# Output tail of a conditioned-attention and recurrence kernel: three parts summed in memory, one more summed by TensorE, and new instruction orders

## What is computed

```
y    = x @ W[itok7].T + b[itok7]                      # a weight matrix per sequence
q,k,v = y @ Wq.T + bq, ...                             # 16 heads of 16
sim  = q.k / (4 * temp)
score = sum over 5 frequencies of alpha * sin(2 pi sim / freq + phi)
w    = sigmoid(score); w = w / sum(w)                  # no softmax
a    = layernorm(w.v @ Wo.T + bo) * gamma + beta
x1   = x + a                                           # residual
h    = relu(x1 @ W1[itok8] + b1); x2 = x1 + h @ W2[itok8] + b2
z    = layernorm(x2) * gamma[itok8] + beta[itok8]
for t in range(32):                                    # over the sequences
    f, i = sigmoid(z[t] @ wf.T + c @ uf.T + bf), sigmoid(... wi, ui, bi)
    c = f * c + i * tanh(z[t] @ wc.T + c @ uc.T + bc)
out  = x1 + tanh(z @ wo.T + c_last @ uo.T + bo)
```

## Time and profile before

| | us |
|---|---|
| median of 3 runs | 320.94 (320.41 to 322.8) |
| the profiled execution | 323.39 |
| its span (first to last instruction) | 321.6 |
| busy: PE, DVE, ACT | 285.4, 274.6, 257.3 |
| granted TensorE clock, mean | 0.983 |

### The profile page before, as it was taken

The page is one execution under the profiler, slowest core; times in us unless marked ns, Lnnn a source line. Parts: engine busy times, 40 slices in busy tenths (PEclk is TensorE's granted clock), DMA queues, the critical chain, the costliest instruction groups (busy, mean ns, idle before and its releaser), DMA issues.

```text
span 321.6 us, 7374 instructions
## 1 busy us (share of the span) xinstructions
PE 285.4 (89%) x2686; PEld 177.5 (55%) x2686; DVE 274.6 (85%) x598; ACT 257.3 (80%) x378; POOL 51.6 (16%) x58
## 2 busy tenths in 40 slices
PE   0787898969889989999999998899999999998971
PEld 0576647866546855554575645556665545543350
DVE  3049996999999999999999998999999998554265
ACT  1069998999999999999999999899999894422132
POOL 5000600041100012332100214140013331210000
PEclk9999997998999999999999999999999999999997
DMA  5698427544044248045445240330444160020007
GB/s 174 244 388 303 93 30 227 116 135 67 0 91 117 30 113 242 0 75 118 103 88 143 74 68 1 71 70 15 108 106 67 35 150 16 2 34 2 0 0 261
DMA packets 32374, 31.97 MB, mean 99 GB/s; under 512 B 10706, under 2 KB 24274, under 8 KB 32338
## 3 DMA queue, kind: packets, MB, share of 16 engines
q1 hardware_dynamic: 27410, 26.67, 29.1%
q0 software_dynamic: 4352, 4.20, 8.7%
q10 hardware_dynamic: 576, 0.64, 0.8%
HBM read 23.36 MB, written 2.10 MB: 79 GB/s over the span
## 4 chain that ended last, share of the span: by engine, by line
DVE 39%; PE 32%; ACT 14%; issue 8%; DMA 3%; POOL 2%; SPq 1%; DVEq 0%; ACTq 0%; POOLq 0%
DVE sc L1626 12%; PE pg L694 7%; DVE ang L1615 5%; PE pg L685 5%; DVE ang L1606 5%; ACT ang L1130 4%; PE pf L491 3%; PE pav L589 3%; ACT ang L1139 3%; PE pf L571 2%; PE pf L547 2%; DVE fc L1761 2%; ACT sc L1121 2%; DMA w<-x 1%; DVE vz L1596 1%
## 5 line engine op out<-in xcount | busy, mean ns | idle before, releaser
L1139 ACT ACTIVATE ang<-ang,qs 128x2560 f32<-128x2560 int32 x32 | 77.4, 2433 | 0.3 <-DVE ang L1615 0.2
L1626 DVE SCALAR_TENSOR_TENSOR sc<-ang,ratio,sc 128x512 f32<-128x512 f32 (+1 forms) x120 | 73.0, 637 | 0.4
L1130 ACT ACTIVATE ang<-sc,phase 128x512 int32<-128x512 f32 (+1 forms) x110 | 64.5, 650 | 0.0
L685 PE MATMUL pg<-gate_w,zT 128*64 128x384 f32 x256 | 50.8, 499 | 0.6 <-DVE zT L1751 0.4
L694 PE MATMUL pg<-gate_u,cT 128*64 128x384 f32 x256 | 47.7, 493 | 1.6 <-DVE cT L1770 1.5
L1615 DVE TENSOR_SCALAR ang<-ang 128x2560 int32<-128x2560 int32 x32 | 47.5, 1501 | 0.0
L1606 DVE TENSOR_SCALAR ang<-sc,phase 128x256 int32<-128x256 f32 (+1 forms) x90 | 32.4, 412 | 2.6 <-ACT sc L1121 2.5
L1179 ACT ACTIVATE gat<-pg 128x384 f32<-128x384 f32 x32 | 15.6, 487 | 22.7 <-PE pg L694 22.3
L694 PEld LDWEIGHTS pg<-gate_u,cT 128*64 128x64 f32 x256 | 16.4, 136 | 22.1 <-issue 15.0
L513 PE MATMUL pf<-wc,xg 128*64 128x256 f32 x128 | 17.1, 416 | 9.5 <-DMA wc<-in_cond 8.8
L1149 ACT ACTIVATE sc<-sc,lead 128x512 f32<-128x512 f32 (+1 forms) x40 | 23.4, 628 | 2.3 <-DVE sc L1626 2.2
(11 more groups left out here) (114 smaller groups left out, 474.1 us busy)
## 6 DMA issues: line engine op xcount, KB each, us to landing
wc<-in_cond SPq DMA_DIRECT2D x30, 257.0 KB, 3.5
w<-in_up SPq DMA_DIRECT2D x32, 128.5 KB, 2.6
wa<-in_down SPq DMA_DIRECT2D x32, 66.0 KB, 1.9
xt<-in_xt SPq DMA_DIRECT2D x8, 256.0 KB, 3.0
xt<-rows POOLq DMA_DIRECT2D x8, 256.0 KB, 4.2
w<-x POOLq DMA_DIRECT2D x8, 256.0 KB, 4.2
xg<-in_x SPq DMA_DIRECT2D x3, 512.0 KB, 5.1
qm<-qT SPq DMA_DIRECT2D x48, 32.0 KB, 2.1
```

The source lines that it names most:

```text
L685: pe.matmul(pg[n % 2][u * L:(u + 1) * L, 0:GCOLS], zT[:, q % 2, kc, t * L:(t + 1) * L], gate_w[:, kc, u, :], start=False, stop=(kc == KC - ...
L1130: op = act.activation(ang[:, n % SLOTS, f, r], unit(n)[:, r], ACT.Identity, scale=TURN / FREQS[f], bias=phase[:, p * NF + f:p * NF + f + 1])
L1139: act.activation(a.bitcast(F32), a, ACT.Sin, scale=2 * PI_LOW / TURN, bias=qs[:, 3:4]).then_inc(sine_ready, 1)
L1626: op = dve.scalar_tensor_tensor(out=unit(n)[:, r], in0=ang[:, n % SLOTS, f, r].bitcast(F32), scalar=ratio[:, p * NF + f:p * NF + f + 1], i ...
```

## The change

Four things change in one step.

- **Tail, in memory.** For parts 0, 5 and 1 (`OUT_DMA`) SP stores x1 into the output inside the recurrence (`store_x1`). At the end the tanh of these parts isn't added to x1 by VectorE: POOL adds it to the output in HBM with an accumulating transfer (`out_added`).
- **Tail, by TensorE.** Part 5 joins parts 6 and 7 as one whose sum with hoc TensorE makes: its kept product is brought back into PSUM (`bring_back`) and `output_sum(5)` adds hoc. The output parts 6 and 7 are made ahead of `state_output` rather than behind it. The order of the tanh is 0, 5, 1, 2, 6, 3, 7, 4.
- **Small moves between engines.** `ON_ACT` loses one angle of the units 10, 12 and 21 and gains one of unit 22, so VectorE makes two angles more. The bias row of part 6 comes from TensorE (`output_bias(6)`) rather than ScalarE. Gate biases by TensorE: cells 13, 21 and 28 added, 17 and 24 taken out.
- **New orders** on all five lists. The 9 rest constants are loaded behind the attention constants and the first weights of group 1, the adapter weights of part 0 behind the second `spread_q`, and `centre_output_weights` on VectorE moves from after the first `divided` to the beginning.

```diff
-BIAS_BY_PE = (0, 1, 2, 4, 6, 8, 10, 12, 14, 16, 17, 18, 24, 31)
-ROW_BY_PE = (0, 1, 2, 3, 4, 5)
+BIAS_BY_PE = (0, 1, 2, 4, 6, 8, 10, 12, 13, 14, 16, 18, 21, 28, 31)
+ROW_BY_PE = (0, 1, 2, 3, 4, 5, 6)
...
-BY_PE = (6, 7)
-BY_DVE = (0, 1, 2, 3, 4, 5)
-TAIL = (0, 1, 2, 3, 4, 5, 6, 7)
+BY_PE = (5, 6, 7)
+BY_DVE = (0, 1, 2, 3, 4)
+OUT_DMA = (0, 5, 1)
+TAIL = (0, 5, 1, 2, 6, 3, 7, 4)
+STORED = tuple(q for q in TAIL if q not in OUT_DMA)
...
+            def store_x1(q):
+
+                added_wait(sp, q)
+                sp.dma_start(out[part(q)].rearrange("u p d -> p u d"), x1[:, part(q)]).then_inc(x1_out, 16)
...
+            def out_added(q):
+
+                pool.wait_ge(x1_out, 16 * len(OUT_DMA))
+                pool.wait_ge(tail_tanh, TAIL.index(q) + 1)
+                pool.dma_start(out[part(q)].rearrange("u p d -> p u d"), kept(q), accum_op=ALU.add).then_inc(summed_out, 16)
...
+            def bring_back(q):
+
+                pe.wait_ge(go_kept, q + 1)
+                pe.wait_ge(s_copied, B)
+                pe.wait_ge(v_ready, NG)
+                pe.matmul(banks[q], eye[:, :], flat(go[:, part(q)]), start=True, stop=False, skip_group_check=True)
...
+            output_part(7, 0)
+            output_part(7, 1)
+            state_turned(31)
+            bring_back(5)
+            state_output()
+            output_sum(5)
+            output_sum(6)
+            output_sum(7)
```

822 lines of the change are left out of this document (409 added, 413 removed).

## The result

| | median | runs | profiled execution | span |
|---|---|---|---|---|
| before, beside after | 321.87 us | 4, 320.41 to 324.05 | 323.39 us | 321.6 us |
| after | 326.9 us | 4, 326.27 to 330.42 | 327.07 us | 325.2 us |

The ratio of after to before on record is 1.0191, 95% interval 1.0136 to 1.0246: some 6 us (4.4 to 7.9). The prediction had nothing, and its range ended at +2.5. Of the forecast cases none happened; the nearest, A, had the right sign and part of the mechanism.

What follows compares the result with a forecast made beforehand. VectorE's work was taken to bound 64 to 263 us, recurrence and TensorE 263 to 308, then VectorE's tail. Terms -1.50 + 0.96 - 0.90 + 1.05 + 0.30 = -0.09 gave 320.8 us from median 320.94; 8-in-10 range 317.2 to 323.4.

Steps and rivals of the forecast that it cites:

- A: Rival at the end: accumulating transfers into HBM take 3.0 us each and land last; +4.7, 325.5 us; chance 0.09.
- First groups, -1.50: Start, 51 to 56 us: centring output weights earlier fills VectorE's hole, so angles start sooner; -1.5 us, bounds 0 and 2.5.
- Two angles, +0.96: 64 to 263 us: net two 128x512 angles move to VectorE, 0.48 us each, lengthening that stretch by 0.96 us.
- POOL's wait goes, -0.90: 64 to 263 us: new orders remove VectorE's one listed wait, for POOL's deviation of part 4; -0.90 us.
- new waits 0: All steps may wait somewhere new under the new orders; taken as 0, with ends of +2 and -1.8 us.
- the prediction's own sign: 64 to 263 us: VectorE idling more than 4 us there would mean the forecast is wrong.
- Warm matmuls, 0: TensorE's early waits: removed or added idle matmuls stand in waits and change nothing.
- End of the recurrence, +1.05: Last cells from 26: TensorE's moved pieces overfill its windows; +1.05 us, between 0.3 and 2.0, including +0.41 for bringing part 5 back.
- The bound of 2.0: End of the recurrence: upper cost in us if weight loads of 0.1 to 0.2 are exposed at each piece.
- Tail, 8.25 us behind hoc: After hoc starts: VectorE's last addition ends 8.25 us later, before 9.05; only 0.8 us of 2.5 dropped comes back.
- Draining, +0.30 together with the tail: Last stores: serial transfers end 12.35 us after hoc starts (T), +0.65; if accumulating costs nothing, -0.8; taken +0.30.

Runs made afterwards that it cites:

- g1: f3 with the angles of units 10 and 12 given back from VectorE to ScalarE; 324.73 us, ratio 1.0069.
- f2: Changed kernel with four places of VectorE's list altered: three normalising steps and a residual moved relative to neighbouring work; 326.40 us, ratio 1.0145.
- f3: f2 with the tail of the kernel before and its order at cell 26, without the gate bias of cell 28 on TensorE; 323.37 us, ratio 1.0055.
- e1: Changed kernel with the whole tail of the kernel before, other new lists kept; 325.04 us, ratio 1.0092.
- g3: Kernel before with only TensorE's part of the new tail, no early stores or accumulating transfers; 323.70 us, ratio 1.0033.
- e2: Kernel before with the whole new tail and early stores, all other lists as before; 324.99 us, ratio 1.0076.
- h3: Kernel before without the two warm matmuls ahead of the first queries; 322.42 us, ratio 1.0010.
- h1: Changed kernel with the two warm matmuls ahead of the first queries put back; 326.31 us, ratio 1.0130.
- h2: f3 with the two warm matmuls ahead of the first queries put back; 322.65 us, ratio 1.0035.
- f4: Kernel before with only parts 0 and 1 stored early and their tanh added by accumulating transfers; 322.71 us, ratio 0.9997.
- g2: Kernel before with unit 24's wrap ahead of part 3's second moments and part 3's normalising ahead of part 4's residual; 322.50 us, ratio 1.0002.
- e4: Changed kernel with output parts 6 and 7 behind state_output and input gates of cells 28 and 31 whole ahead of the turn; 326.85 us, ratio 1.0126.

## Why the prediction was wrong, point by point

- *First groups, -1.50.* Right in place, and at first larger than predicted: the first large angle starts at 52.90 us instead of 56.26, unit 4's sine 2.2 us sooner (59.60 for 61.79). But the lead is gone by cell 26: 289.23 in both profiles. It was a lead over an order that then had less idle time. This and the next two points are the largest miss: ahead of cell 26 the prediction's terms come to -1.44 us, and it was +1.4 to +2.5.
- *Two angles, +0.96.* g1 found nothing of it, within its noise. A cost per instruction holds only while that engine is the bound.
- *POOL's wait goes, -0.90; new waits 0.* This step failed, and the prediction's own sign of it came: VectorE idled 5.6 us from 64 to 263, where over 4 was to mean a wrong forecast. The wait of part 4 only moved, and three more of over 0.5 us for POOL came, 0.93 + 0.71 + 0.59 + 0.62 = 2.85 us for 0.90, and one of 1.01 us for the adapter's accumulating transfer of part 5 (0.60 to 1.03 in eight of the ten profiles of the changed lists, in none of the six of the lists of before):

```profile
248.49 0.69 DVE L1737 TENSOR_TENSOR w<-pr,w 128x512 f32<-128x512 f32 x1 [1.01 <-DMA w<-x]
```

  The orders were on the table: a wrap behind `moments(0, 1)` could be read from the list, and the wait of the earlier trace rows itself had such a wrap ahead of it (POOL's instruction took 1.35 us at 195.87 in the kernel before, 0.22 at 82.87). I put the wait down to an order and asked neither why POOL was late nor what work stood between it and the step that waits. How much of the 1.4 to 2.5 us this is: f2 gives 0.46% by ratios (1.5 us), 0.9 by the medians and 0.5 us by the profile, f3 against e1 some 0.9 us beside cell 26. I estimate 0.5 to 1.5 us from these; none of them is clear of the noise by itself.
- *Warm matmuls, 0.* Failed in kind: where the clock had risen by then, they kept it up. In size it is 0.3 to 1.0 us by the medians, not clear of the noise.
- *End of the recurrence, +1.05.* The way of counting was right, the sizes too small, and with them one step wrong in kind: 2.46 us. Half an output part is 1.06 us, taken as 0.86; half of the input gates 0.80, taken as 0.64. Together they were to fit the first window, at nothing; they overran it by 0.41 us at two cells. Cell 28's second half costs 0.19, as predicted, and the last cell, with its half of the gates and part 7, 0.57 for 0.36. The order at cell 26 costs 0.53 behind the turn (22.32 for 21.79; a net 0.25 by e1), taken as 0.1. `bring_back` was right: hoc followed the last turn by 2.21 us where it was 1.86, +0.35 for +0.41. The bound of 2.0 that I gave for exposed loads of weights was still too low.
- *Tail, 8.25 us behind hoc.* 7.93, right.
- *Draining, +0.30 together with the tail.* Failed in size. One transfer after the other was to end the data at T + 12.35, and I then took less than half of the +0.65. The last full window ends at 324, T + 12.45, but 28% of the next is still used, so the data ends near T + 12.7 by the measure that gave 11.7 before; the trace's last packet ends at T + 12.96 (T + 11.71 in the kernel before). That the serial count comes near is in part luck: it had 1.55 us for an accumulating transfer, which was 1.86, and its first data at T + 3.85, which was T + 4.3, and the engines' share went up to 1.19 in a window, where it had counted 1. From hoc to the end of the span it is 13.65 us where it was 12.51, +1.14. The rule of the Trainium skill that the prediction quoted, "DMA: Bandwidth & Descriptors", section "Issuing engines are not separate DMA queues", that all transfers end up on the same 16 engines, made it +0.65 and was the better number; the trace agrees, with stores landing in 5.2 us beside accumulating transfers where they took 2.3 without.
- *Rival A.* It had the accumulating transfers land last. The third lands at T + 12.43, 8.4 us after its issue, and the last store, which shares the engines with it, at T + 13.28. They take 1.86 us each, above the 1.6 from which the rival was to decide and far from its 3.0. Of its 4.7 us, 0.7 to 1.0 came (T + 12.7 to 12.96 for T + 12.0).
- *The range.* Its upper end, 323.4, is 0.3 us more than its own terms give (320.8 + 0.95 + 0.35 + 1.0 = 323.1); the result lies outside by either.

Sum by the runs, in per cent of the time. By the runs alone each difference is near its noise; the profiles behind the turn of cell 26 bear out the first three, and the last two stand on the runs: TensorE's pieces 0.3 (g3), accumulating transfers 0.4 (e2 less g3), order at cell 26 0.1 (e1, net), the four places 0.3 to 0.5 (f3, f2), warm 0.1 to 0.3 (h3, h1 and h2, by their medians). Together 1.2 to 1.6 of 1.9 (1.6 by the medians). What h2 still has, 0.35% (0.05 to 0.66) or about 1 us (0.6 by the medians), stays open: it lies ahead of cell 26, in lists that differ at some hundred places, and no single one was found for it. The wait for part 5's transfer, 0.73 us in h2, is a candidate, which wasn't tried apart.

No kernel that ran beats the kernel before; f4, g2 and h3 equal it within what the runs tell.

## What to carry to other kernels

An engine at 98% of a stretch is a statement on one order. When an order changes, don't price only the work moved: for each step that waits on another engine, ask what now runs *beside* the small instruction it waits for, and how much of its own work stands between. Where a full window is to take one more piece, measure the piece by its starts in a full stretch. And when work is moved to the DMA engines at the end of a program, price the end of the data, not the end of the compute: what VectorE saved here (1.1 us behind hoc) the engines took back twice (2.3 us).

## What was not expected of the hardware

- A GpSimd `tensor_scalar` on 128x2 numbers takes 0.22 us alone (276.87 in the kernel before), 0.62 beside a VectorE sum of 128x512 with two inputs in SBUF, 1.36 beside an int32 `tensor_scalar` of 128x2560, and 2.02 beside the end of such a sum and then the other; behind the int32 one it ends within 0.1 us.
- Three accumulating transfers of 256 KB into HBM, issued 0.75 us apart, land after 4.4, 6.2 and 8.4 us beside stores (median 4.6 for the eight `w<-x` into SBUF of the same profile), and double the landing time of the stores beside them, from 2.3 and 2.9 to 5.2 and 5.8 us.
- An idle gap of 0.89 us ahead of the first queries, 15 us into the program, was followed by a stretch at the lower clock in six of nine executions; f3 kept full level with the same list, and in e4 and g1 the trace has its first entry, at full level, only 5.2 to 5.5 us later.
- The first 20 us have two paces of their own: in some executions four queries' matmuls take 2.01 us, in others 1.13, from the same list, and everything behind shifts by 1.4 us (first sine at 27.13 or 25.73 with the lists of the kernel before). The column shows 1.00 in both, but the trace's first entry at full level is at 17.11 us in the one and at 12.9 in the other, and the two times are about as far apart as the keys' 1.91 and 1.03 us, where the column did show 0.50 and 1.00. So the slow pace is most likely the lower level, without an entry.
